# Two sixteen-head attentions, the seam behind the latent attention, and the end of an eight-sublayer kernel in a new form

## What is computed

```python
x = x + tanh(g_xattn[0]) * L0_xattn(layernorm(x), ctx, ctx)     # a0: 16 heads of 8, window of 64, mask
x = x + tanh(g_ffn[0])   * L0_ffn(layernorm(x))                 # f0: top 2 of 8 experts
x = x + tanh(g_xattn[1]) * L1_xattn(ctx, layernorm(x))          # a1: latent attention, 8 heads of 64
x = x + tanh(g_ffn[1])   * L1_ffn(layernorm(x))                 # f1: top 2 of 16 experts + a shared expert
x = x + tanh(g_xattn[2]) * L2_xattn(layernorm(x), ctx)          # a2: 16 heads of 8, with q, k, v projections
x = x + tanh(g_ffn[2])   * L2_ffn(layernorm(x))                 # f2: receptance layer
x = x + tanh(g_xattn[3]) * L3_xattn(layernorm(x), ctx, ctx)     # r3: correlation and roll
x = x + tanh(g_ffn[3])   * L3_ffn(layernorm(x))                 # f3: top 2 of 8 experts, GELU

# L0_xattn and L2_xattn, for each entry and each of 16 heads (DH = 8):
scores = q @ k.T / sqrt(DH)          # a0: -inf where |i - j| > 64
y      = softmax(scores) @ v
```

## Time and profile before

| | |
|---|---|
| median of 3 runs | 1036.71 us |
| the three runs | 1033.21, 1036.71, 1041.0 us |
| the profiled execution | 1029.27 us |
| its span in the trace | 1027.5 us |
| its mean granted TensorE clock | 0.877 of full speed |
| a0, then f0 | 18 to 172 us, 172 to 262 us |
| a1, then f1 | 265 to 516 us, 538 to 591 us |
| a2, then f2 | 593 to 739 us, 739 to 778 us |
| r3, then f3 | 780 to 894 us, 894 to 1003 us |
| end | 1003 to 1027.5 us |

### The profile page before, as it was taken

How to read it: one execution, slowest core, us unless ns; L and a number is a source line. 1 busy time by engine, 2 the same in 40 slices (tenths; PEclk the granted TensorE clock), 3 DMA queues, 4 the chain that set the end, 5 groups by cost and what they waited for, 6 DMA issues and landing times. The chain is left out here.

```text
span 1027.5 us, 20832 instructions
## 1 busy us (share of the span) xinstructions
PE 832.6 (81%) x5994; PEld 592.8 (58%) x6008; DVE 635.2 (62%) x1905; ACT 503.7 (49%) x1419; POOL 424.3 (41%) x721
## 2 busy tenths in 40 slices
PE   4999994994789999999879849998697548489990
PEld 1465662663557777777647626666466326267770
DVE  5799972333366777877544358998598347434442
ACT  1466671553156566666516517776534113145551
POOL 2356653002343556653330065663155208513343
PEclk9999996998689999999989958999858765579995
DMA  8999701331000000000015410000001221111114
GB/s 283 378 407 372 253 23 51 75 76 37 11 11 7 15 20 22 23 17 7 17 33 118 114 32 17 21 19 7 1 1 43 82 63 46 55 41 56 51 37 130
DMA packets 68860, 78.92 MB, mean 77 GB/s; under 512 B 12432, under 2 KB 58144, under 8 KB 68496
## 3 DMA queue, kind: packets, MB, share of 16 engines
q1 hardware_dynamic: 59840, 62.74, 19.0%
q0 software_dynamic: 6368, 13.38, 4.5%
q10 hardware_dynamic: 2544, 1.48, 0.6%
HBM read 31.61 MB, written 45.96 MB: 75 GB/s over the span
## 5 line engine op out<-in xcount | busy, mean ns | idle before, releaser
L320 POOL DMA_INDIRECT routed_region<-routed_lines,line_slots x96 | 96.5, 1005 | 32.4 <-issue 21.9
L352 POOL DMA_INDIRECT late_results<-routed_region,line_slots x64 | 63.6, 993 | 78.1 <-DVE work L635 62.0
L887 PE MATMUL banks<-work,weights_a 128*128 128x128 f32 x512 | 78.8, 300 | 14.0 <-ACT work L1115 8.2
L255 POOL TENSOR_TENSOR small<-small,half_and_eps 128x1 f32<-128x1 f32 x144 | 85.2, 591 | 11.3
L769 ACT ACTIVATE probs_keymajor<-banks 128x512 f32<-128x512 f32 x128 | 70.1, 595 | 37.0 <-PE banks L565 37.0
L1324 PE MATMUL banks<-weights_f,exps 128*128 x156 | 85.3, 630 | 1.1 <-ACT exps L1374 0.9
L539 PE MATMUL banks<-work 32*128 32x512 f32 x256 | 81.0, 712 | 0.0
L640 DVE TENSOR_REDUCE small<-banks 128x8 f32<-128x1024 f32 x64 | 77.6, 1213 | 5.5 <-PE banks L539 5.3
L649 DVE TENSOR_TENSOR exps<-banks,small 128x1024 f32<-128x1024 f32 x64 | 77.8, 1215 | 3.7 <-PE banks L565 3.4
L887 PEld LDWEIGHTS banks<-work,weights_a 128*128 128x128 f32 x512 | 66.4, 203 | 23.3 <-ACT work L1115 10.3
L1478 DVE TENSOR_TENSOR work<-exps,banks 128x64 f32<-128x64 f32 (+1 forms) x86 | 26.8, 312 | 78.2 <-ACT exps L1380 77.1
(11 more groups left out here) (278 smaller groups left out, 2014.9 us busy)
## 6 DMA issues: line engine op xcount, KB each, us to landing
routed_region<-mid SPq DMA_DIRECT2D x52, 528.0 KB, 14.4
exps<-routed_region SPq DMA_DIRECT2D x125, 66.0 KB, 1.9
routed_region<-work SPq DMA_DIRECT2D x86, 64.0 KB, 1.8
weights_f<-in_weights_f SPq DMA_DIRECT2D x1, 4096.0 KB, 16.6
weights_f<-in_weights_f SPq DMA_DIRECT2D x3, 1024.0 KB, 11.5
shifted_rows<-work SPq DMA_DIRECT2D x16, 128.0 KB, 1.7
work<-expert_results SPq DMA_DIRECT2D x4, 512.0 KB, 5.7
routed_region<-routed_lines,line_slots POOLq DMA_INDIRECT x96, 2.4
```

The source lines that it names most:

```text
L255: nc.gpsimd.tensor_tensor(rstd[:, s, 1:2], rstd[:, s, 0:1], k.half[:, 0:1], ALU.pow).then_inc(sem.rstd, 1)
L320: nc.gpsimd.indirect_dma_start(k.regions[layer % 2], bass.IndirectOffsetOnAxis(k.slots[:, b, j:j + 1], 0), k.line[:, b % LINES, j, :], Non ...
L352: nc.gpsimd.indirect_dma_start(k.late[:, b % 2, j, :], None, k.regions[layer], bass.IndirectOffsetOnAxis(k.slots[:, b, j:j + 1], 0)).then_ ...
L887: last = nc.tensor.matmul(bank[:, MA, p * T:(p + 1) * T], k.w[weight][:, p * 128:(p + 1) * 128], kvT[:, sl, part * T:(part + 1) * T], star ...
```

## The change

1. **Sixteen-head attentions.** `scores` is one stage: in a0 four masks, then four products on the four groups of rows into the four banks. It waits for `shift` and for the first exponential of the entry before. The first eight heads are no longer shifted by DVE: DVE writes minus the scaled maximum (128x8, `nmx`), and ACT takes eight exponentials of 128x128 straight from banks 0 and 1 with that column as the bias (`exps(0)`). Heads 9 to 16 go as before, but in an exponential of 1024 columns of their own (`exps(1)`). All lists of a0 and a2 have a new order and new lags. In a2 `fetched` runs two rounds ahead of the addition where it ran one ahead.
2. **Seam a1 to f1.** The shared expert leaves the walks of DVE and ACT. In PE's walk there remain single products: gate 0, up 0 and gate 1 in the rounds of the last entry; the others stand in `tensor()` between the steps of the table, and silu, multiplication and addition behind those steps on ACT and DVE.
3. **Row numbers.** SP reads the first eight row numbers before it waits for the sent rows, not after (f0, f1, f3).
4. **End.** Results are read and written in 8 transfers of two entries. Of each pair DVE multiplies and adds the first entry; for the other ACT writes the product into a bank and DVE adds it. POOL adds nothing. The last two blocks are opened with `no_gpsimd_drain=True`, and PE clears f3's semaphores, 24 of them, behind its last product.

```diff
@@ small_head_attention: tensor
-                def stage(b, sl):
-                    wait(pe, s.q, b + 1)
-                    wait(pe, s.keys, b + 1)
-                    wait(pe, s.shifted, b * 2 + (first // 2 - 1))
...
+            def scores(b, sl):
+                wait(pe, s.q, b + 1)
+                wait(pe, s.keys, b + 1)
+                wait(pe, s.exp, b * 2 - 1)
+                wait(pe, s.shifted, b)
+                if masked:
+                    for g in range(NG):
+                        nc.tensor.matmul(bank[:, g, :], k.maskb[:, 0:128], k.maskb[:, 128:], start=True, stop=False)
+                for g in range(NG):
...
+                last.then_inc(s.scores, 1)
@@
-            walk(pe, [(out_T, 5), (scores(0), 2), (qkv, 1), (out, 5), (pv, 4), (scores(2), 2),
-                  (probs(0), 3), (output_transpose, 4), (probs(2), 3), (in_T, 0)]
+            walk(pe, [(probs(2), 4), (scores, 2), (qkv, 1), (pv, 4), (out, 5), (output_transpose, 4),
+                      (probs(0), 3), (out_T, 4), (in_T, 0)]
                  if project else
-                 [(scores(0), 1), (in_T, 0), (logits, 6), (probs(0), 3), (output_transpose, 4), (probs(2), 3),
-                  (ranks, 6), (out_T, 4), (scores(2), 1), (out, 4), (pv, 3), (next_T, 5)])
+                 [(scores, 1), (in_T, 0), (logits, 6), (probs(0), 3), (output_transpose, 4), (probs(2), 3),
+                  (ranks, 6), (out_T, 4), (out, 4), (pv, 3), (next_T, 5)])
@@ vector
+                    if half == 0:
+                        wait(dve, s.max, b * 2 + 1)
+                        nc.vector.tensor_scalar(nmx[:, sl, :], mx[:, sl, part], -SCALE, None, ALU.mult).then_inc(s.nmax, 1)
@@
+            def shift(b, sl):
+                wait(dve, s.max, b * 2 + 2)
+                wait(dve, s.ptr, b * NG - NG)
+                nc.vector.tensor_tensor(split(k.e[:, sl, 1024:2048], T),
+                                        bank[:, 2:4, :].rearrange("p g (j t) -> p (g j) t", j=HG),
+                                        over(mx[:, sl, 8:16], T, 2), ALU.subtract).then_inc(s.shifted, 1)
@@
-            walk(dve, [(shift(1), 4), (norm_in, 1), (stats_in, 0), (maximum(0), 3), (add, 6), (shift(0), 3),
-                  (values, 2), (maximum(1), 3), (divide, 5)]
+            walk(dve, [(maximum(0), 3), (values, 2), (add, 6), (maximum(1), 3), (divide, 5), (norm_in, 1),
+                       (shift, 3), (stats_in, 0)]
                  if project else
-                 [(norm_out, 8), (stats_in, 0), (add, 7), (maximum(1), 4), (stats_out, 7), (shift(1), 4),
-                  (chosen, 8), (maximum(0), 3), (divide, 6), (norm_in, 1), (shift(0), 3), (placed, 8)])
+                 [(shift, 4), (add, 7), (stats_out, 7), (placed, 9), (stats_in, 0), (norm_out, 7), (norm_in, 1),
+                  (maximum(0), 3), (chosen, 8), (divide, 6), (maximum(1), 3)])
@@ gpsimd
-            walk(pool, [(fetched, -1), (dev_in, 0), (spread_values, 3), (spread_keys, 1), (bias, 4)]
+            walk(pool, [(spread_values, 4), (spread_keys, 3), (bias, 4), (dev_in, 2), (fetched, 0)]
...
@@ scalar
+            def exps(half):
+                def stage(b, sl):
+                    if half == 1:
+                        wait(act, s.shifted, b + 1)
+                        nc.scalar.activation(k.e[:, sl, 1024:2048], k.e[:, sl, 1024:2048], ACT.Exp, scale=SCALE).then_inc(s.exp, 1)
+                        return
+                    wait(act, s.nmax, b + 1)
+                    wait(act, s.ptr, b * NG - NG)
+                    for h in range(8):
+                        last = nc.scalar.activation(k.e[:, sl, h * T:(h + 1) * T],
+                                                    bank[:, h // HG, (h % HG) * T:(h % HG + 1) * T], ACT.Exp,
+                                                    bias=nmx[:, sl, h:h + 1], scale=SCALE)
+                    last.then_inc(s.exp, 1)
+                return stage
@@
-            walk(act, [(queries, 1), (outputs, 4), (probs_out, 3), (in_T, 0), (out_T, 4), (exps, 2)]
+            walk(act, [(probs_out, 3), (in_T, 0), (exps(1), 2), (out_T, 4), (queries, 0), (outputs, 3),
+                       (exps(0), 1)]
                  if project else
-                 [(out_T, 5), (exps, 3), (next_T, 6), (outputs, 4), (queries, 0), (logits, 6), (probs_out, 3)])
+                 [(queries, 0), (probs_out, 3), (out_T, 4), (exps(0), 1), (next_T, 5), (outputs, 3), (exps(1), 1),
+                  (logits, 5)])
@@ latent_attention: tensor (DVE and ACT lose their stage `shared`)
-            walk(pe, [(out, 4), (k_ctx, 1), (probs(0), 3), (k_rot, 1), (probs(2), 3), (next_T, 5), (k_lat, 1),
+            walk(pe, [(out, 4), (shared_gate(0), 4), (k_ctx, 1), (probs(0), 3), (k_rot, 1), (probs(2), 3), (next_T, 5), (k_lat, 1),
                       (logits, 5), (query, 1), (pv, 3), (values(0), 1), (ranks, 6), (scores(0), 1), (values(1), 1),
-                      (scores(1), 1), (in_T, 0), (shared, 7)])
+                      (scores(1), 1), (in_T, 0), (shared_up, 4), (shared_gate(1), 5)])
@@ expert_layer: sync
+        sp.wait_ge(s.steps, LINES_AT)
+        rows_ = list(registers(mybir.EngineType.SP, row_i[:, 0:8], REGIONS[layer % 2] * SHARE - T))
         for slot in range(LINES):
             sp.wait_ge(ld.sent[slot], lines_sent(layer + 1, slot))
-        sp.wait_ge(s.steps, LINES_AT)
-        rows_ = []
@@
-            for q in range(4):
-                sp.dma_start(tile.both[:, 4 * q:4 * q + 4, :, :],
...
+            for q in range(B // 2):
+                sp.dma_start(tile.both[:, 2 * q:2 * q + 2, :, :],
...
@@ expert_layer: tensor
         if shared:
-            pe.wait_ge(routed.kept, B)
-            pe.wait_ge(s.sh, 2)
-            shared_in(pe, 3, "sh_gate", 0, s.sg)
+            shared_up(pe, 1)
...
+            shared_up(pe, 2)
+            shared_down(pe, 0)
+            shared_gate(pe, 3)
+            shared_down(pe, 1)
+            shared_up(pe, 3)
             shared_down(pe, 2)
             shared_down(pe, 3)
-            pe.wait_ge(s.sadd, 4)
@@ expert_layer: tensor, behind the last block
+        if layer == 2:
+            sems.clear_own(pe)
@@ expert_layer: scalar, vector, gpsimd at the end
+                    nc.scalar.activation(scaled[:, q, j, :], tile.both[:, 2 * q + 1, j, :], ACT.Copy,
+                                         scale=k.shares[:, j, 2 * q + 1:2 * q + 2]).then_inc(s.scaled, 1)
...
+                    v.scalar_tensor_tensor(own, tile.both[:, 2 * q, j, :], k.shares[:, j, 2 * q:2 * q + 1], own,
+                                           ALU.mult, ALU.add).then_inc(s.summed, 1)
+                    dve.wait_ge(s.scaled, 2 * q + 2)
...
+                    v.tensor_tensor(other, scaled[:, q, j, :], other, ALU.add).then_inc(s.summed, 1)
...
-                        nc.gpsimd.tensor_tensor(k.x[:, b, :], tile.both[:, b, j, :], k.x[:, b, :],
-                                                ALU.add).then_inc(s.summed2, 1)
@@ roll block, last block
-    with nc.Block() as block:
+    with nc.Block(no_gpsimd_drain=True) as block:
...
-                sp.wait_ge(ld.out, 64)
+                sp.wait_ge(ld.out, 128)
```

More of the change, by code:

```diff
@@ L557, in stage @@
                 def stage(b, sl):
-                    wait(pe, s.exp, b + 1)
+                    wait(pe, s.exp, b * 2 + (first // 2 + 1))
                     for g in range(first, first + 2):
@@ L759, in _ @@
         def _(act):
-            def exps(b, sl):
-                wait(act, s.shifted, b * 2 + 2)
-                nc.scalar.activation(k.e[:, sl, :], k.e[:, sl, :], ACT.Exp, scale=float(1 / np.sqrt(DH))).then_inc(s.exp, 1)
+            def exps(half):
[12 more added lines that the diff above has]
+                return stage
             def probs_out(b, sl):
@@ L793, in queries @@
                     wait(act, s.xTp, b + 1)
-                wait(act, s.scores, b * 2 - 2)
+                wait(act, s.scores, b - 1)
                 if project:
@@ L1167, in expert_layer @@
     if layer == 2:
[L1168 to L1170 removed]
+        (s.b2, s.to, s.scaled, s.summed) = sems.new(tag, "b2 to scaled summed", True)
+        both = sems.new(tag, "both0 both1 both2 both3 both4 both5 both6 both7", True)
     got, put = ld.got, ld.put
@@ L1327, in hidden_T @@
         def hidden_T(m):
+            if shared and m == 0:
+                pe.wait_ge(s.sadd, 4)
             pe.wait_ge(s.hid, m + 1)
@@ L1364, in scalar @@
         if shared:
-            shared_silu(act, 3)
-            act.wait_ge(s.sy, 4)
+            for q in range(4):
+                shared_silu(act, q)
         if layer == 2:
@@ L1376, in nonlinear @@
         def nonlinear(m):
+            if shared and m == 0:
+                act.wait_ge(s.sh, 4)
             act.wait_ge(s.up, m + 1)
@@ L1382, in hidden_T @@
         def hidden_T(m):
+            if shared and m == 0:
+                act.wait_ge(s.sy, 4)
             act.wait_ge(s.hT, m + 1)
@@ L1411, in scalar @@
             act.wait_ge(s.share, SHARE_ALL)
-            for q in range(4):
```

(9 more changed lines are left out.)

126 lines of the change are left out of this document (54 added, 72 removed).

## The result

| | before | changed |
|---|---|---|
| median | 1036.47 us (4 runs, 1033.21 to 1041.0) | 1022.1 us (4 runs, 1019.37 to 1023.71) |
| profiled execution, its span | 1029.27, 1027.5 us | 1023.71, 1021.9 us |
| ratio | | 0.9856, 95% interval 0.9811 to 0.9901 |

The kernel is 1.4% faster, 14 us in the medians; 13 were forecast. The sum is right. Of its five terms the two for the attentions are not, and two later measurements of the same kernel gave 0.9925 on a faster chip and 0.9866 on one like the first.

The account below looks back on a forecast made before the run. PE and DVE together were taken to bound a0 and a2. +2 - 5 - 4 - 0.7 - 5.2 = -13 against the 1036.71 us median gave 1023; the forecast's own range was 1015 to 1032, the whole range 1008 to 1041.

Parts of the forecast that it names:

- A round of a0, 7.94: In a0, a round set by a circle of waits across PE and ACT takes 7.94 us, against 8.00 before.
- rivals A: In a0 and a2, the four products run as two pairs in series: +33 over 31 rounds, about 1056; chance 0.12.
- D: In a0 and a2, products 0.22 and exponentials 0.27 longer: +8 to +15, 1031 to 1038; chance 0.14.
- B with the round: Rounds go by engine sums, not the circle: 7.2 in a0, 6.9 in a2, about 1008; chance 0.10.
- the prediction's own sign: The forecast is wrong if an a0 round is over 8.3 or under 7.5, or the drain turns up elsewhere.
- Two prices: In a0 and a2, four products side by side take 1.06 and eight exponentials 2.17, by this trace's rows.
- a0 in all, +2: a0 with its seam gets 2 us longer, range -1 to +4.
- then -1 in 15 rounds, -1 at the drain: In a0, after +4 in the first three rounds, 15 rounds save 1 us and the last entry's shorter exponentials 1.
- a2, -5: a2 gets 5 us shorter, range -8 to +2: 15 rounds of 7.2 against 7.38 give -2.7, fill and drain -2.
- Seam, -4: At the seam a1 to f1, the first turn comes 4 us earlier, bounds -1.5 and -5.
- Row numbers, -0.7: At the seam r3 to f3, SP's load of 0.53 and the queue steps around it leave the chain: -0.7 us.
- End, -5.2: At the end, additions finish 1.5 later but POOL's drain of 6.58 goes: -5.2 us, from -3.5 to -6.5.

Follow-up runs that it names:

- chip A: The chip on which the kernel before took 1022 to 1023 us in two sessions; the changed kernel's ratio there was 0.9925.
- the early masks: Changed kernel with a0's masks of banks 2 and 3 issued before the wait for the first exponential: 0.9869, again 0.9832 (1005.32 us), to the kernel before.
- the control on A: The changed kernel, unchanged, timed again on chip A against the kernel before: 1015.89 us, ratio 0.9925.
- on B: The chip on which the kernel before took 1040 us; the changed kernel took 1025.06 us there, ratio 0.9866.

## Why the prediction was right

In part by luck: two terms failed, by 8 us together on chip A, two others were too careful by 3 to 4, and where the 14 were measured, the kernel before runs slow for a reason that no trace names. By its own steps, with what traces and runs gave:

- **A round of a0, 7.94:** measured 7.97. Four products 1.07 (taken: 1.06), eight exponentials 2.19 (2.17). The circle is shown by the early masks. That it came out so close is in part cancelling: masks and products took 2.02 (taken: 2.10), the way back to the exponentials 3.51 (3.61), but exponentials and the signal to the masks 2.44 (2.23), since PE starts 0.25 behind the last exponential and not 0.06. With this, rivals A and D fall, and B with the round (its time should have read about 1006, not 1008). In a round of the control on A PE is busy for 6.65 us (forecast 6.7), ACT for 6.46 (6.6), DVE for 6.72 (6.3). By the prediction's own sign, a round over 8.3, it failed on B: four rounds of the first profile are 8.46 to 9.60, only one of them with a lowered clock.
- **Two prices.** On both the rows of this kernel were right. From the Trainium skill, "TensorE: Matmul & The Clock Gate", Part 3, "Measured speedup vs the span model", I had estimated 1.28 for the four products; they took 1.07, so here four together ran 3.7 times as fast as one after the other (4 x 0.98 / 1.07), not 3.07 times. From the Trainium skill, "ScalarE: Activation LUTs", "What ACT_TABLE_LOAD costs", I had estimated 2.44 for the eight exponentials; they took 2.19.
- **a0 in all, +2** (its own terms add up to +1.4): this step failed, in "then -1 in 15 rounds, -1 at the drain". In the trace of the changed kernel on A the first probabilities are transposed at 38.53 instead of 34.63, so the fill is 3.9 (taken: 4), but the 15 rounds to the last entry's take 117.6, where they took 116.6: +1, since several of the old a0's first and last rounds were shorter than 8 (7.1 to 7.6) and I compared with its steady one. From there to f0 it is 23.2 in both: no gain at the emptying of the pipeline. That makes 4.8, above my range; the old a0 with everything else new was 8 us faster in time. On B the attentions cost nothing that can be measured against the old: there the old a0 was slow too in the one trace of it that is surely from B (f0 at 180.4, with rounds up to 9.7).
- **a2, -5:** failed. The circle was mis-sized by 0.2 at the step from the evictions to the scores (1.85 against 1.65) and 0.1 each at qkv and `outputs`, while the exponentials took 0.2 less: 7.42 against 7.2, and the rounds before had been 7.38 (the prediction's 4.57 on the way should read 4.47; its 7.2 stands). Fifteen rounds, first eviction to that of the last entry, took 108.9 to 111.6 with the new form and 106.5 to 110.0 with the old. Nor was the fill shorter: from a2's first fetch to the first eviction it is 26.6 to 26.7, where it was 26.2 to 26.4. Only what lies behind the last entry got some 2 us shorter, on average.
- **Seam, -4:** 5 to 6. The mechanism was right, and so was what is late next: PE's shared products hold the first turn. What I had left out is the 1.9 us in a1's last round.
- **Row numbers, -0.7:** the first turn of f3 came 5.15 behind the last sending, and now 4.6 to 4.9, but 5.5 in one trace.
- **End, -5.2:** 7.2 in the traces, outside my range. The first results were there 1.4 sooner after their issue (2.8 against 4.2; I had 0.4 to 0.7), and 32 additions took 0.267 each instead of 0.29 to 0.335, so the additions ended 0.9 sooner behind the last sending than POOL's had (13.7 against 14.6), where I had them 1.5 later. The price of the drain was right; that it must be taken away by the flag was not.

So on chip A the forecast had a0 and a2 together some 8 us too good, and the seam and the end 3 to 4 too bad; there 7.2 us were measured, and the forecast of 13 would have been 6 too high. In the first measurement and on B 14 to 15 were measured: against A the kernel before takes 14 to 17 us longer there, the changed one only 6 to 9. The forecast knew nothing of that: it was worked out from a profile in which the old a0 isn't slow (f0 at 174.5, as on A), and held against that profile the changed kernel's first one gains 5.6, not 13. The hit on the medians is luck to that extent.

## What to carry to other kernels

When both busy engines of a pipeline are relieved, draw the circle of waits that is left before counting a gain. Then look at the instructions right behind a wait in that circle: those that need only part of what it waits for (two masks of four) can go ahead of it. Compare a new steady round with the mean of all old rounds, the first and last among them. Work given to an engine near the end also delays whatever that engine must do at the end.

## What I had not expected

- The same two kernels differ by 7 us on A and by 14 to 15 on B and in the first measurement. In the traces from there rounds of 8.2 to 9.7 stand among those of 7.97 and 8.00, in both forms of a0. Most of them come while the experts' weights are loaded (DMA share 1.03, 404 GB/s in the window from 74 to 83), but the load isn't the cause by itself: the control on A has 1.03 and 405 GB/s in the same window and no long round, and the same holds for the profile before (1.02 and 404). I have only the idle gaps; the cause stays open.
- POOL's drain took 6.6 to 7.0 us both behind sixteen additions and behind an indirect transfer.
- Four products on four groups of 32 rows took 1.07 at a granted clock of 1.00, and 2.02 at 0.50 in the fill (36.24 to 38.26 in the control on A); a single one over 128 rows took 0.98 at 1.00.
